# Moving score banks, one V product and one statistics step in a four-layer transformer kernel

## The chip, the cores and the metric

The kernel runs on one core of a Trainium2 chip. The metric is the device time of one execution in microseconds, the median of several runs. Short names: PE is TensorE (PEld its weight loads), DVE is VectorE, ACT is ScalarE, POOL is GpSimd, SP the queue that issues the transfers.

## The reference, cut to what matters

Sixteen sequences of 256 tokens with 256 features go through four layers, each a conditioned attention block and a conditioned MLP block. Layer 1 is causal, layer 3 rotates q and k and has a gated MLP, layers 2 and 3 have biases on q, k and v.

```
for layer in (L0, L1, L2, L3):
    h = norm(x) * (1 + scale1) + shift1          # per sequence
    q, k, v = h @ Wq, h @ Wk, h @ Wv             # 16 heads of 16 features
    a = softmax(q @ k.T / 4)                     # layer 1: causal mask
    x = x + gate1 * ((a @ v) @ Wo)
    h = norm(x) * (1 + scale2) + shift2
    x = x + gate2 * (act(h @ W1 + b1) @ W2 + b2)
```

## The kernel before, in words

The program is a pipeline over 64 tiles (4 layers times 16 sequences; tile n is sequence n mod 16 of layer n // 16). `steps` runs a body for t = -2 to 65. In a step, tile t+1 (`s.q`) gets its q, k and v, tile t (`s.a`) its attention, tile t-1 (`s.r`) its output projection and second norm, and tile t-2 (`s.m`) its MLP. Of each layer the steps 3 to 13 are a hardware loop (`Fori`), the others are written out. Each engine runs its own instructions in the order of the code and waits on semaphores.

Within a step PE does the MLP of tile t-2 interleaved with the untransposed scores of tile t (`score_pair`, from which DVE takes the maxima), then `query`, `key`, and then the part that this document is about. There, the sixteen heads of tile t are done again as transposed scores: eight `transposed_pair`s, two at a time; the exponentials of ACT (L893, one per head, 512 columns, 384 in the causal layer) read them from the PSUM bank that `ST_BANKS` names for the head, and write the tile `PR`; `outputs(g)` multiplies the exponentials of heads 4g to 4g+3 with V (L701). Between them stand `values(0)` and `values(1)`, the two halves of the V projection of tile t+1, and `norm_2`, the transposes of the second norm of tile t-1. The order before, outside the last layer:

`transposed_pairs(0, 1)`, `maxima_to_rows(1)`, `key(0)`, `key(1)`, `transposed_pairs(2, 3)`, `outputs(0)`, `transposed_pairs(4, 5)`, `values(0)`, `outputs(1)`, `norm_2`, `transposed_pairs(6, 7)`, `outputs(2)`, `values(1)`, `outputs(3)`.

PSUM has 8 banks of 512 columns. `banks_free` makes PE wait for the exponential of the last head that used the bank (`ac_exp`), or, for a bank that had other contents, for the engine that reads those. Before, heads 0 to 7 use banks 4, 5, 0, 7 twice, and heads 8 to 15 use 4, 5, 1, 3 twice, so heads 2 and 3 and heads 6 and 7 share banks 0 and 7. q is projected into bank 1, k into bank 3, v into bank 2; DVE evacuates them (`split_q` and `split_k` at L1315 to L1327, `values_out` at L1230). `up(j)` of the MLP takes banks 3 and 2 in turn.

DVE does after the last maxima: `split_q`, `split_k` (each a high part and a low part), `statistics_2` of the second norm (L935, L940), `normalise_2` (L948), which waits for the reciprocal root from POOL (L1358, L1360), `modulate_2` (L1116, L1125), then the evacuations of `outputs` (L1222) and of V (L1230). POOL makes the low part of the second norm's features from `modulate_2` (L1440), for which the first `up` of the next step waits. SP moves the rows of maxima into QS (L1484), for which pairs 0 and 4 wait, and stacks q and k into QS and KS (L1518).

Of the kernel before, what the change touches and what calls it, by code (L numbers as in the profile page):

```python
# [25 lines left out]
ACT = mybir.ActivationFunctionType  # L26
# [44 lines left out]
WO_BANK = 6  # L71
NORM1_BANK = 6

ST_BANKS = ((4, 5, 0, 7) * 2 + (4, 5, 1, 3) * 2, (4, 5, 0, 7) * 2 + (4, 5, 0, 1) * 2)
NORM2_BANK = (0, 7)
PARTNER = [i ^ HG for i in range(32)]

# [7 lines left out]
def build(nc, a, out):  # L85
    ctx = ExitStack()
    with ctx:
# [243 lines left out]
        def apart(eng):  # L331

            eng.nop(nofuse=True)

        def hidden_hi(eng, s, j):

            if s.lm == ROPE:
                eng.wait_ge(dv_gh, NJ * (s.m - NSEQ * ROPE) + j + 1)
            else:
                eng.wait_ge(ac_g, NJ * s.m + j + 1)  # L340
# [26 lines left out]
        def _(pe):  # L367
# [77 lines left out]
            def body(s):  # L445
# [49 lines left out]

                def up(j):

                    m, dst = s.m, bank(3 - j % 2)
                    x = H1 if isinstance(m, int) and m == NTILE - 1 else H2
                    if j == 0:  # L500
                        if x is H1:
                            pe.wait_ge(dv_g, NJ * (m - NSEQ * ROPE))
                        weights(s.lm, "1", s.sm, *((0, 4, 2, 6) if s.lm == ROPE else (0, 2)))
                        pe.wait_ge(dv_h2, m + 1)
                        pe.wait_ge(po_h2, m + 1)
                        key_read(s)
                    elif j == 1:
                        at_least(pe, dv_v, s.nq)
                    elif s.lm == ROPE:
                        pe.wait_ge(dv_g, NJ * (m - NSEQ * ROPE) + j - 1)  # L510
                    else:
                        pe.wait_ge(ac_g, NJ * m + j - 1)
                    if j == NJ // 2:
                        weights(s.lm, "1", s.sm, *((1, 5, 3, 7) if s.lm == ROPE else (1, 3)))
                    last = project(dst[:, 0, :], cols(W1, j * P), x)
                    if s.lm == ROPE:
                        last = project(dst[:, 1, :], cols(W1, DFF + j * P), x)
                    last.then_inc(pe_up, 1)
# [57 lines left out]
                def norm_2():  # L576

                    if s.a is not None:
                        pe.wait_ge(ac_exp, H * s.a + last_user(ST_BANKS[rope][0:HB] + (NORM2_BANK[rope],), HB) + 1)
                    pe.wait_ge(dv_xn2, s.r + 1)  # L580
                    to_features(bank(NORM2_BANK[rope]), TOK).then_inc(pe_h2, 1)

# [28 lines left out]
                def values(i):  # L611

                    if s.q is None:
                        return
                    if scored and i == 0:
                        pe.wait_ge(dv_max, H * (s.a + 1))
                    elif i == 0:
                        hidden_read(s)
                        at_least(pe, dv_v, s.nq)
                    for k in range(KD):  # L620
                        last = product(bank(2)[:, i, :], [x[:, k, i * P:(i + 1) * P] for x in H1],
                                       [w[:, k, 2 * D:3 * D] for w in wq], k == 0, k == KD - 1)
                    if i == NT - 1:
                        last.then_inc(pe_v, 1)
# [26 lines left out]
                def banks_free(p):  # L651

                    a_, banks = s.a, ST_BANKS[rope]
                    if p % HQ == 0:
                        pe.wait_ge(sp_mt[p // HQ], 16 * (a_ + 1))
                    for h in (2 * p, 2 * p + 1):
                        before = last_user(banks, h)
                        if before is not None:
                            pe.wait_ge(ac_exp, H * a_ + before + 1)
                        elif banks[h] in (0, 4, 5):  # L660
                            pe.wait_ge(dv_max, H * a_ + last_user(S_BANKS + (banks[h],), H) + 1)
                        elif banks[h] == 7:
                            at_least(pe, dv_dn, s.m_done)
                        elif banks[h] == 1 and rope:
                            pe.wait_ge(dv_rot, 2 * (s.q - NSEQ * ROPE) + 1)
                        elif banks[h] == 1:
                            at_least(pe, dv_q, s.q_done)
                        elif banks[h] == 3:
                            at_least(pe, dv_k, s.q_done)

                def transposed_pair(p):

# [101 lines left out]
                if scored:  # L774
                    transposed_pairs(2, 3)
                    outputs(0)
                    transposed_pairs(4, 5)
                    values(0)
                    if rope and s.r is not None:
                        norm_2()  # L780
                    outputs(1)
                    if not rope and s.r is not None:
                        norm_2()
                    transposed_pairs(6, 7)
                    if rope:
                        values(1)
                    outputs(2)
                    if not rope:
                        values(1)
                    outputs(3)  # L790
                else:
                    values(0)
                    values(1)
                    if s.r is not None and not s.tail:
                        norm_2()
# [10 lines left out]
        def _(ac):  # L806
# [24 lines left out]
            def body(s):  # L831
# [18 lines left out]
                for j in range(NJ) if s.m is not None else ():  # L850
# [7 lines left out]
                    at_least(ac, po_gl, NJ * m + j + 1 - RING)  # L858
                    if s.lm == ROPE:

                        nc.scalar.activation(G[:, j % RING, :], bank(3 - j % 2)[:, 1, :], ACT.Silu,
                                             bias=VEC[:, ROPE, V_B1 + NJ + j:V_B1 + NJ + j + 1]).then_inc(ac_g, 1)
                    else:

                        at_least(ac, pe_dn, NJ * m + j + 1 - RING)
                        for dst in (G, GH[0]):
                            last = nc.scalar.activation(dst[:, j % RING, :], bank(3 - j % 2)[:, 0, :], ACT.Gelu,  # L867
                                                        bias=VEC[:, s.lm, V_B1 + j:V_B1 + j + 1])
                        last.then_inc(ac_g, 1)
                    if j == 1:  # L870
# [61 lines left out]
        def _(dv):  # L932
# [85 lines left out]
            def body(s):  # L1018
# [16 lines left out]
                def hidden(j):  # L1035
                    m = s.m
                    if s.lm == ROPE:
                        dv.wait_ge(ac_g, NJ * m + j + 1)
                        nc.vector.scalar_tensor_tensor(G[:, j % RING, :], bank(3 - j % 2)[:, 0, :],  # L1039
                                                       VEC[:, ROPE, V_B1 + j:V_B1 + j + 1], G[:, j % RING, :],  # L1040
                                                       ALU.add, ALU.mult).then_inc(dv_g, 1)
                        dv.wait_ge(dv_g, NJ * (m - NSEQ * ROPE) + j + 1)
# [181 lines left out]
                def values_out():  # L1224
# [2 lines left out]
                        return  # L1227
                    dv.wait_ge(pe_v, s.q + 1)
                    at_least(dv, po_v, s.nq)
                    nc.vector.tensor_copy(VT[:], bank(2)).then_inc(dv_v, 1)  # L1230

                if s.tail:
                    return
# [20 lines left out]
                    evacuate(1)  # L1254
                else:
                    split_q()
                    split_k()
                    if s.lr != ROPE:
                        statistics_2()
                    normalise_2()  # L1260
                    modulate_2()
                    evacuate(0)
# [394 lines left out]
```

## Time and profile before

| | us |
|---|---|
| median of 3 runs | 2203.06 (2202.44 to 2203.37) |
| the profiled execution | 2201.76 |
| its span | 2199.6 |

| engine | busy us | share of the span |
|---|---|---|
| PE | 2124.3 | 97% |
| PEld | 1794.6 | 82% |
| DVE | 1711.1 | 78% |
| ACT | 1250.9 | 57% |
| POOL | 1043.9 | 47% |

The granted clock of TensorE is 0.99 of full speed over the span. Matmuls overlap in the pipeline and their ends are modelled, so PE's busy share hides short waits; they are read from the distances between the starts of matmuls and loads. The idle time in brackets behind a load is the time in which no load ran, which is also there when the matmuls before it take long, so it is compared with the same kind of place elsewhere.

### The profile page before, as it was taken

The page shows a single profiled execution, that of the slowest core. Times are in us where ns is not written, and L with a number is a line of the kernel's source. Part 1 is how long each engine was busy: PE and PEld are TensorE (multiplying, and loading weights), DVE is VectorE, ACT ScalarE, POOL GpSimd, SP SyncE. Part 2 cuts the span into 40 slices and gives each one's busy share as a digit, 9 for nine tenths or more (in the row PEclk, how much of TensorE's full clock was granted, in tenths as well). Part 3 has the DMA queues.
Part 4 walks back from the last instruction along what each step waited for, and adds up shares of the span by engine and source line. Part 5 has one row for each costly group of instructions (what it writes and reads, how often), then busy time and mean ns, then how long its engine had stood idle before and what let it go on. Part 6 is the DMA issues. An engine that isn't in the chain of part 4 may idle for free.

```text
span 2199.6 us, 63077 instructions
## 1 busy us (share of the span) xinstructions
PE 2124.3 (97%) x20080; PEld 1794.6 (82%) x20080; DVE 1711.1 (78%) x4340; ACT 1250.9 (57%) x2618; POOL 1043.9 (47%) x1300
## 2 busy tenths in 40 slices
PE   5899999999999999999999999999999999999998
PEld 4688888888888888888878887888888888888887
DVE  5677777777777777777777777777999898989884
ACT  1566666666655555555676666666655454444543
POOL 2345544555554455445455544545553434344433
PEclk8899999999999999999999999999999999999999
DMA  6421222222222212212332121122221212121210
GB/s 214 154 67 64 68 72 67 63 75 86 91 71 72 69 61 67 72 63 81 104 96 64 66 76 62 58 72 83 72 95 57 74 53 72 57 69 57 69 63 25
DMA packets 164143, 166.11 MB, mean 76 GB/s; under 512 B 28672, under 2 KB 143232, under 8 KB 164032
## 3 DMA queue, kind: packets, MB, share of 16 engines
q1 hardware_dynamic: 164032, 164.69, 23.3%
q8 instruction: 63, 1.03, 0.2%
q14 instruction: 48, 0.39, 0.1%
HBM read 58.47 MB, written 4.39 MB: 29 GB/s over the span
## 4 chain that ended last, share of the span: by engine, by line
PE 74%; DVE 12%; issue 5%; ACT 2%; POOL 2%; SPq 2%; DMA 1%; DVEq 0%; ACTq 0%; POOLq 0%
PE B L371 31%; PE B L532 14%; PE B L701 8%; PE B L678 6%; PE B L476 6%; DVE NEGM L1032 4%; PE B L541 4%; PE B L551 2%; ACT PR L893 2%; PE B L635 2%; PE B L449 2%; SPq L1518 2%; DVE ST L935 1%; DVE G L1039 1%; POOL GHl L1397 1%
## 5 line engine op out<-in xcount | busy, mean ns | idle before, releaser
L893 ACT ACTIVATE PR<-B 128x512 f32<-128x512 f32 (+1 forms) x1024 | 504.7, 571 | 284.1 <-PE B L678 279.2
L1397 POOL TENSOR_TENSOR GHl<-G,GHh 128x256 fp32r<-128x256 f32 x512 | 377.5, 738 | 452.2 <-ACT GHh L867 282.1
L1032 DVE TENSOR_REDUCE NEGM<-B 128x2 f32<-128x512 f32 x768 | 485.2, 682 | 80.4 <-PE B L476 80.3
L371 PE MATMUL B<-H2h,W1h 128*128 128x256 f32 x1248 | 387.7, 311 | 1.9 <-DVE VT L1230 1.2
L371 PE MATMUL B<-H2h,W1l 128*128 128x256 f32 x1248 | 353.4, 283 | 0.0
L371 PE MATMUL B<-H2l,W1h 128*128 128x256 f32 x1248 | 352.7, 283 | 0.0
L867 ACT ACTIVATE G<-B,VEC 128x256 f32<-128x256 f32 x384 | 182.0, 474 | 274.7 <-PE B L371 274.7
L532 PE MATMUL B<-W2h,GHh 128*128 128x256 f32 x1024 | 296.9, 290 | 4.4 <-POOL GHl L1397 2.9
L532 PE MATMUL B<-W2l,GHh 128*128 128x256 f32 x1024 | 290.1, 283 | 0.0
L532 PE MATMUL B<-W2h,GHl 128*128 128x256 f32 x1024 | 289.3, 283 | 0.0
L371 PEld LDWEIGHTS B<-H2h,W1h 128*128 128x128 f32 x1248 | 237.3, 190 | 43.6 <-issue 23.8
L701 PE MATMUL B<-PR,V 128*32 128x256 f32 (+1 forms) x4096 | 260.9, 373 | 5.9 <-ACT PR L893 1.9
L371 PEld LDWEIGHTS B<-H2l,W1h 128*128 128x128 f32 x1248 | 238.2, 191 | 0.0
L371 PEld LDWEIGHTS B<-H2h,W1l 128*128 128x128 f32 x1248 | 237.2, 190 | 0.0
L678 PE MATMUL B<-QS,KS 64*128 64x256 f32 (+1 forms) x2048 | 200.5, 307 | 12.1 <-DMA QS<-MT 4.6
L678 PEld LDWEIGHTS B<-QS,KS 64*128 64x128 f32 x2048 | 142.8, 188 | 80.1 <-ACT PR L893 36.0
L532 PEld LDWEIGHTS B<-W2h,GHh 128*128 128x128 f32 x1024 | 195.4, 191 | 14.0 <-POOL GHl L1397 3.8
L476 PE MATMUL B<-KS,QS 48*128 48x256 f32 (+1 forms) x2048 | 194.9, 309 | 10.5 <-DVE NEGM L1032 5.5
L1029 DVE CUSTOM_DVE_ANT_0 B<-B,MASK 128x128 f32<-128x128 f32 (+1 forms) x512 | 165.8, 390 | 39.6 <-PE B L476 39.6
L532 PEld LDWEIGHTS B<-W2h,GHl 128*128 128x128 f32 x1024 | 195.9, 191 | 0.0
L532 PEld LDWEIGHTS B<-W2l,GHh 128*128 128x128 f32 x1024 | 195.9, 191 | 0.0
L701 PEld LDWEIGHTS B<-PR,V 128*32 128x32 f32 x4096 | 108.3, 110 | 89.9 <-ACT PR L893 19.6
(177 smaller groups left out, 4671.2 us busy)
## 6 DMA issues: line engine op xcount, KB each, us to landing
QS<-QHL SPq DMA_DIRECT2D x768, 64.0 KB, 2.1
KS<-KHL SPq DMA_DIRECT2D x768, 64.0 KB, 2.1
GA<-gate_scratch SPq DMA_DIRECT2D x48, 256.0 KB, 3.2
GM<-gate_scratch SPq DMA_DIRECT2D x48, 256.0 KB, 3.3
RAW<-in_w SPq DMA_DIRECT2D x36, 256.0 KB, 3.2
GA<-in_rows_last SPq DMA_DIRECT2D x16, 256.0 KB, 3.1
GM<-in_rows_last SPq DMA_DIRECT2D x16, 256.0 KB, 3.1
out<-X SPq DMA_DIRECT2D x16, 256.0 KB, 2.2
```

The source lines that it names most:

```text
L371: last = nc.tensor.matmul(dst, w[i], x[j], start=(first_k and n == 0), stop=(last_k and n == 2))
L449: return nc.tensor.matmul(dst, IDENTB[:], MASK[:, 1], start=True, stop=False, skip_group_check=True)
L476: last = nc.tensor.matmul(bank(banks[h])[:, i, 0:keys], QS[b:b + STK, p, i * P:(i + 1) * P], KS[b:b + STK, p, 0:keys], start=True, stop=True)
L532: last = nc.tensor.matmul(bank(7)[:, i, :], GH[x][:, j % RING, i * P:(i + 1) * P], W2[y][:, j, :], start=(j == 0 and n == 0 and i == 0), s ...
L541: last = nc.tensor.transpose(dst[:, f, i * P:(i + 1) * P], src[:, i, f * P:(f + 1) * P], IDENT[:])
L678: last = nc.tensor.matmul(B[:, banks[h], k * T:k * T + T - first], KS[b:b + ROWS, p, k * P:(k + 1) * P], QS[b:b + ROWS, p, first:T], start ...
L701: last = nc.tensor.matmul(bank(6 + g // 2)[32 * j:32 * j + 32, g % 2, c], V[:, k, HV * h:HV * h + 32], PR[:, h % PRING, k, 0:n], start=(k ...
L867: last = nc.scalar.activation(dst[:, j % RING, :], bank(3 - j % 2)[:, 0, :], ACT.Gelu, bias=VEC[:, s.lm, V_B1 + j:V_B1 + j + 1])
L893: nc.scalar.activation(PR[:, h % PRING].rearrange("p k q -> p (k q)")[:, 0:n], src[:, 0:n], ACT.Exp, scale=SCALE).then_inc(ac_exp, 1)
L1029: last = nc.vector.tensor_tensor_reduce(src[:, i, 0:keys], src[:, i, 0:keys], unmasked, -1.0, HIGHEST, ALU.add, ALU.min, NEGM[:, i, c:c + 1])
L1032: last = nc.vector.tensor_reduce(NEGM[:, :, c], src, op=ALU.max, axis=AX.X, negate=True)
L1397: nc.gpsimd.tensor_tensor(GH[1][:, j % RING, :], G[:, j % RING, :], GH[0][:, j % RING, :].bitcast(F32), ALU.subtract).then_inc(po_gl, 1)
```

## The change

Four things, all of them outside the last layer (`rope` and `s.la == ROPE` keep the code before; the last attention step, t = 63, takes the new banks too, since it has no next tile):

- Banks: the heads 0 to 15 use 4, 5, 0, 7, 4, 5, 1, 2, and the same again. Heads 4 to 7 go to 4, 5, 1, 2 and wait for exponentials 0 and 1 and for q's evacuation from bank 1. `norm_2`, in bank 0, now waits for exponential 10.
- `values(0)` stands behind `outputs(1)`, and V is projected into bank 3, where k was, with a wait for k's evacuation (`dv_k`).
- `up(j)` takes banks 2 and 3 in turn, not 3 and 2; the wait for k's evacuation moves from `up(0)` to `up(1)`.
- `statistics_2` stands between `split_q` and `split_k` on DVE.

```
-ST_BANKS = ((4, 5, 0, 7) * 2 + (4, 5, 1, 3) * 2, (4, 5, 0, 7) * 2 + (4, 5, 0, 1) * 2)
+ST_BANKS = ((4, 5, 0, 7, 4, 5, 1, 2) * 2, (4, 5, 0, 7) * 2 + (4, 5, 0, 1) * 2)
+V_BANK = (3, 2)
...
+        def up_bank(s, j):
+
+            return 3 - j % 2 if s.la == ROPE else 2 + j % 2
...
-                        key_read(s)
+                        if s.la == ROPE:
+                            key_read(s)
                     elif j == 1:
+                        if s.la != ROPE:
+                            key_read(s)
                         at_least(pe, dv_v, s.nq)
...
-                        pe.wait_ge(ac_exp, H * s.a + last_user(ST_BANKS[rope][0:HB] + (NORM2_BANK[rope],), HB) + 1)
+                        pe.wait_ge(ac_exp, H * s.a + last_user(ST_BANKS[rope][0:12] + (NORM2_BANK[rope],), 12) + 1)
...
-                    if scored and i == 0:
+                    if i == 0 and rope:
                         pe.wait_ge(dv_max, H * (s.a + 1))
                     elif i == 0:
+                        pe.wait_ge(dv_k, s.q + 1)
+                    if i == 0 and not scored:
                         hidden_read(s)
                         at_least(pe, dv_v, s.nq)
...
-                        elif banks[h] == 3:
-                            at_least(pe, dv_k, s.q_done)
+                        elif banks[h] == 2:
+                            pe.wait_ge(dv_max, H * (a_ + 1))
...
                     transposed_pairs(4, 5)
-                    values(0)
-                    if rope and s.r is not None:
-                        norm_2()
+                    if rope:
+                        values(0)
+                        if s.r is not None:
+                            norm_2()
                     outputs(1)
-                    if not rope and s.r is not None:
-                        norm_2()
+                    if not rope:
+                        values(0)
+                        if s.r is not None:
+                            norm_2()
...
                     split_q()
-                    split_k()
                     if s.lr != ROPE:
                         statistics_2()
+                    split_k()
                     normalise_2()
```

PE, in the loop of the first layer, before: heads 4 and 5, heads 6 and 7, and the first product with V (QS,KS are transposed scores, PR,V the product with V, IDENT,TOK `norm_2`, WQ0h,H1h the V projection).

```order
L678 MATMUL B<-QS,KS 128x256 [waits ac_exp]
L678 MATMUL B<-QS,KS 128x256 x3
L659 REGISTER_ALU
L678 MATMUL B<-QS,KS 128x256 [waits ac_exp]
L678 MATMUL B<-QS,KS 128x256 x3
L691 REGISTER_ALU [waits po_v,ac_exp]
```

The same place in the changed kernel:

```order
L688 MATMUL B<-QS,KS 128x256 [waits ac_exp]
L688 MATMUL B<-QS,KS 128x256 x3
L688 MATMUL B<-QS,KS 128x256 [waits dv_max,dv_q]
L688 MATMUL B<-QS,KS 128x256 x3
L701 REGISTER_ALU [waits po_v,ac_exp]
```

The second pair (heads 6 and 7) no longer waits for an exponential, but for DVE. PE a little later in the same step, before: heads 10 and 11, then the V projection's six products (the last is shown), the second product with V, and `norm_2`.

```order
L678 MATMUL B<-QS,KS 128x256 [waits dv_k,dv_q]
L678 MATMUL B<-QS,KS 128x256 x3
L371 MATMUL B<-WQ0h,H1h 128x256 [waits dv_max]
...
L371 MATMUL B<-WQ0h,H1l 128x256
L701 MATMUL B<-PR,V 32x256 [waits ac_exp]
L701 MATMUL B<-PR,V 32x256 x7
L579 REGISTER_ALU
L541 MATMUL B<-IDENT,TOK 128x128 [waits dv_xn2,ac_exp]
```

The same place in the changed kernel:

```order
L688 MATMUL B<-QS,KS 128x256 [waits ac_exp]
L688 MATMUL B<-QS,KS 128x256 x3
L711 MATMUL B<-PR,V 32x256 [waits ac_exp]
L711 MATMUL B<-PR,V 32x256 x7
L376 MATMUL B<-WQ0h,H1h 128x256 [waits dv_k]
...
L376 MATMUL B<-WQ0h,H1l 128x256
L549 MATMUL B<-IDENT,TOK 128x128 [waits dv_xn2,ac_exp]
```

The product with V now directly follows the transposed scores, and `norm_2` the V projection. DVE in the same loop, before: the two halves of `split_k` and then `statistics_2` and `normalise_2`.

```order
L1327 TENSOR_TENSOR QHL<-B,QHL 128x512 [waits dv_qh]
L1325 CAST KHL<-B 128x512 [waits sp_stk1,sp_stk0,pe_k]
L1327 TENSOR_TENSOR KHL<-B,KHL 128x512 [waits dv_kh]
L935 ISA [waits po_x1]
L935 BN_STATS ST<-X 128x6
...
L940 BN_AGGR MV<-ST 128x2
L948 TENSOR_SCALAR TOK<-X,MV,RS 128x256 [waits po_x2,po_rs2]
```

The same place in the changed kernel:

```order
L1340 TENSOR_TENSOR QHL<-B,QHL 128x512 [waits dv_qh]
L948 ISA [waits po_x1]
L948 BN_STATS ST<-X 128x6
...
L953 BN_AGGR MV<-ST 128x2
L1338 CAST KHL<-B 128x512 [waits sp_stk1,sp_stk0,pe_k]
L1340 TENSOR_TENSOR KHL<-B,KHL 128x512 [waits dv_kh]
L961 TENSOR_SCALAR TOK<-X,MV,RS 128x256 [waits po_x2,po_rs2]
```

The statistics stand ahead of k's evacuation instead of behind it. The instructions of ACT, POOL and SP and their waits are the same in both kernels.

## Rows read from the trace of the kernel before

**Rows 1.** Windows, busy time in one step of layer 0: PE, PEld, DVE, ACT, POOL, clock.
```profile
287.50:318.82 31.32, 31.06 (x299) 26.03 (x297) 23.38 (x46) 20.07 (x43) 15.80 (x19) 1.00 0.21 68
```
**Rows 2.** Timeline, PEld, same step: start, length, instructions [idle before, releaser].
```profile
309.82 0.30 PEld L678 LDWEIGHTS B<-QS,KS 64*128 64x128 f32 x4
310.41 0.33 PEld L678 LDWEIGHTS B<-QS,KS 64*128 64x128 f32 x4 [0.29 <-ACT PR L893]
...
311.87 0.53 PEld L678 LDWEIGHTS B<-QS,KS 64*128 64x128 f32 x8 [0.41 <-ACT PR L893]
312.54 0.19 PEld L371 LDWEIGHTS B<-WQ0h,H1h 128*128 128x128 f32 x1
...
313.45 0.59 PEld L701 LDWEIGHTS B<-PR,V 128*32 128x32 f32 x16
314.45 0.42 PEld L541 LDWEIGHTS B<-IDENT,TOK 128*128 128x128 f32 x4 [0.41 <-ACT PR L893]
315.03 0.54 PEld L678 LDWEIGHTS B<-QS,KS 64*128 64x128 f32 x8 [0.17 <-issue]
...
317.77 0.59 PEld L701 LDWEIGHTS B<-PR,V 128*32 128x32 f32 x16 [0.29 <-ACT PR L893]
318.77 0.19 PEld L371 LDWEIGHTS B<-H2h,W1h 128*128 128x128 f32 x1 [0.41 <-issue]
```
**Rows 3.** Timeline, ACT, same step, exponentials 2 and 3, 5 and 6, 7, 12 to 15.
```profile
309.25 1.04 ACT L893 ACTIVATE PR<-B 128x512 f32<-128x512 f32 x2
...
310.86 1.08 ACT L893 ACTIVATE PR<-B 128x512 f32<-128x512 f32 x2
...
311.81 0.62 ACT L893 ACTIVATE PR<-B 128x512 f32<-128x512 f32 x1
...
315.65 2.07 ACT L893 ACTIVATE PR<-B 128x512 f32<-128x512 f32 x4 [1.10 <-PE B L678]
```
**Rows 4.** Timeline, PEld, a step of layer 2: the transposes of `norm_2`.
```profile
1274.59 0.42 PEld L541 LDWEIGHTS B<-IDENT,TOK 128*128 128x128 f32 x4 [0.75 <-ACT PR L893]
```
**Rows 5.** Timeline, DVE, the same step of layer 2.
```profile
1268.56 0.88 DVE L1320 SCALAR_TENSOR_TENSOR QHL<-B,VEC,QHL 128x256 fp32r<-128x256 f32 x2
1269.73 0.88 DVE L1315 TENSOR_SCALAR KHL<-B,VEC 128x256 fp32r<-128x256 f32 x2 [0.29 <-PE B L371]
...
1271.44 0.74 DVE L935 BATCH_NORM_STATS2 ST<-X 128x6 f32 x2
...
1273.73 0.73 DVE L948 TENSOR_SCALAR TOK<-X,MV,RS 128x256 f32 x2 [1.20 <-POOL RS L1360]
```
**Rows 6.** Timeline, PEld, a step of layer 1: masks of heads 4 to 7 and 8 to 11.
```profile
819.78 0.12 PEld L449 LDWEIGHTS B<-MASK,IDENTB 128*128 128x128 bf16 x2
820.15 0.13 PEld L449 LDWEIGHTS B<-MASK,IDENTB 128*128 128x128 bf16 x2 [0.25 <-ACT PR L893]
...
821.95 0.34 PEld L449 LDWEIGHTS B<-MASK,IDENTB 128*128 128x128 bf16 x4 [0.27 <-ACT PR L893]
```
**Rows 7.** Timeline, PE, layer 3: V projection's first product, `norm_2`, `outputs(1)`.
```profile
1776.16 0.39 PE L371 MATMUL B<-WQ1h,H1h 128*128 128x256 f32 x1
...
1776.98 0.60 PE L541 MATMUL B<-IDENT,TOK 128*128 128x128 f32 x4
1777.50 1.07 PE L701 MATMUL B<-PR,V 128*32 128x256 f32 x16
```
**Rows 8.** Waits of PE in layer 2, 1053.67 to 1533.44 us: total, times, longest.
```profile
PE B L541 <- DVE TOK L948: 4.8, 15, 0.7
```
**Rows 9.** Timeline, SP: the second rows of maxima. Tile QS: issue to landing.
```profile
308.95 0.56 SPq L1484 DMA_DIRECT2D QS<-MT  x1
...
DMA to landing us min/median/max: 2.0/2.1/2.4
```
**Rows 10.** Timeline, POOL, the step of Rows 2: low part for the next `up`.
```profile
317.08 1.28 POOL L1440 TENSOR_TENSOR H2l<-HF,H2h 128x512 fp32r<-128x512 f32 x1 [3.56 <-DVE H2h L1125]
```
**Rows 11.** Timeline, PE, last attention step (t = 63): `outputs(3)`.
```profile
2154.18 1.07 PE L701 MATMUL B<-PR,V 128*32 128x256 f32 x16 [0.91 <-ACT PR L893]
```

More of the change, by code:

```diff
@@ L496, in up @@
                 def up(j):
-                    m, dst = s.m, bank(3 - j % 2)
+                    m, dst = s.m, bank(up_bank(s, j))
                     x = H1 if isinstance(m, int) and m == NTILE - 1 else H2
@@ L620, in values @@
                     for k in range(KD):
-                        last = product(bank(2)[:, i, :], [x[:, k, i * P:(i + 1) * P] for x in H1],
+                        last = product(bank(V_BANK[rope])[:, i, :], [x[:, k, i * P:(i + 1) * P] for x in H1],
                                        [w[:, k, 2 * D:3 * D] for w in wq], k == 0, k == KD - 1)
@@ L859, in body @@
                     if s.lm == ROPE:
-                        nc.scalar.activation(G[:, j % RING, :], bank(3 - j % 2)[:, 1, :], ACT.Silu,
+                        nc.scalar.activation(G[:, j % RING, :], bank(up_bank(s, j))[:, 1, :], ACT.Silu,
                                              bias=VEC[:, ROPE, V_B1 + NJ + j:V_B1 + NJ + j + 1]).then_inc(ac_g, 1)
@@ L866, in body @@
                         for dst in (G, GH[0]):
-                            last = nc.scalar.activation(dst[:, j % RING, :], bank(3 - j % 2)[:, 0, :], ACT.Gelu,
+                            last = nc.scalar.activation(dst[:, j % RING, :], bank(up_bank(s, j))[:, 0, :], ACT.Gelu,
                                                         bias=VEC[:, s.lm, V_B1 + j:V_B1 + j + 1])
@@ L1038, in hidden @@
                         dv.wait_ge(ac_g, NJ * m + j + 1)
-                        nc.vector.scalar_tensor_tensor(G[:, j % RING, :], bank(3 - j % 2)[:, 0, :],
+                        nc.vector.scalar_tensor_tensor(G[:, j % RING, :], bank(up_bank(s, j))[:, 0, :],
                                                        VEC[:, ROPE, V_B1 + j:V_B1 + j + 1], G[:, j % RING, :],
@@ L1229, in values_out @@
                     at_least(dv, po_v, s.nq)
-                    nc.vector.tensor_copy(VT[:], bank(2)).then_inc(dv_v, 1)
+                    nc.vector.tensor_copy(VT[:], bank(V_BANK[s.lq == ROPE])).then_inc(dv_v, 1)
                 if s.tail:
```

## The prediction, made before the changed kernel was run

> **What bounds the kernel now.** I read first the busy times, then one step in the timeline of each layer, then who waits for whom. PE is the bound outside the last layer: in one step of layer 0 of 31.32 us it is busy for 31.06, at the full clock (1.00, which is 2.4 GHz), while DVE has 23.38 and ACT 20.07 [rows 1]. So a gain can only come from waits that the busy share hides, or from fewer changes of PE's way of working. To find them, the starts of the loads are compared with each other. An idle figure in brackets is no wait by itself: 0.41 us stand behind every product with V, since its short loads are through before its matmuls are. The waits in the part that changes are these. Heads 6 and 7 wait for exponential 3 (their banks are those of heads 2 and 3): the load at 310.41 has 0.29 us of idle time ascribed to ACT [rows 2]. `outputs(3)` waits for exponential 15, 0.29 us [rows 2]. In layer 2, `norm_2` has 0.75 us of idle time where layer 0 has 0.41 [rows 2, 4]: 0.34 us more, and in that layer the waits list has PE waiting for DVE's normalised tokens in 15 of 16 steps [rows 8]. The last layer keeps its code, so its part of the time only shifts.
>
> **The change, part by part, on the step of layer 0.** Two distances are needed first. From the end of an exponential to what waits for it: exponential 3 ends at 309.25 + 1.04 = 310.29 and the scores' load starts at 310.41, 0.12 later; exponential 15 ends at 315.65 + 2.07 = 317.72 and the load of `outputs(3)` starts at 317.77, 0.05 later [rows 2, 3].
>
> Banks. Heads 4 and 5 start at 309.82 as before; heads 6 and 7 follow at once, for banks 1 and 2 are free (the last maximum is already waited for by `maxima_to_rows(1)`; q's evacuation I check below). Two pairs take 312.54 - 311.87 = 0.67, so `outputs(0)` starts at 310.49, and a product with V takes 314.45 - 313.45 = 1.00 [rows 2]. PE is at heads 8 to 11 at 311.49 instead of 311.87. They now wait for exponential 5, which starts at 310.86 and takes 0.60 to 0.62; with 0.12 that is 311.6 [rows 3]. Their rows of maxima were sent at 308.95 and such transfers land after 2.0 to 2.4 us, by 311.35 [rows 9]: in time. They end at 311.6 + 0.67 = 312.27.
>
> Order. Now `outputs(1)` comes at once, and needs exponential 7. It starts at 311.81 and ends at 312.43 [rows 3], and nothing that moves is ahead of it: ACT has run without a break since its copy of the maxima. `outputs(1)` is the same kind of load as `outputs(3)`, so I take 0.05, not 0.12: it starts at 312.48. So of the 0.38 us that the banks give, 0.21 are lost again to a new wait. Then 1.00 for the product, 313.48 for `values(0)`, and 0.82 from there to the transposes, as in the last layer where these two stand in this order [rows 7]; before, the V projection took 313.45 - 312.54 = 0.91 to the product behind it. This 0.09 is a change of mode less: projection and transposes both use the whole array, while scores use half of its rows and the product with V quarters of its columns. `norm_2` starts at 314.30; from it to the next block it is 0.52 behind a projection [rows 7] and 0.58 behind a product with V [rows 2]; I take 0.55. So heads 12 to 15 start at 314.85 instead of 315.03. Their exponentials move along with them, and with them `outputs(3)` and the next step: **0.18 us less per step**. The cover holds: the next `up` needs POOL's low part, done at 317.08 + 1.28 = 318.36 against a start at 318.77 [rows 2, 10], and both move by 0.15 to 0.18. Layer 0 has 15 steps like this (t = 1 to 15): 15 x 0.18 = 2.7 us.
>
> The Trainium skill says in "TensorEngine Tiling (Array Packing)", Key Properties, that a change of the tiling mode, not of the tile, drains the array. By that rule alone, at the 0.09 us of the rows and with four changes of mode before and three after, a step would gain 0.09 and 46 steps 4.1 us; the waits are the larger part of my sum.
>
> Layer 1 (causal). Before, the masks of heads 4 to 7 take from 819.78 to 820.28, 0.50 us, those of heads 8 to 11 only 0.34 [rows 6]: 0.16 us of waiting for exponential 3, which goes. The exponentials have 384 columns there and end sooner against PE, so I expect no new wait, and the change of mode adds 0.09: 0.25 us in 16 steps, 4.0 us. If the new wait takes all of the 0.16, it is 1.4.
>
> Statistics between the splits, layer 2. q's low part ends at 1268.56 + 0.88 = 1269.44. Before, k's split starts at 1269.73, the statistics at 1271.44, and they are done 1.20 us ahead of the 1273.73 at which DVE normalises, so at 1272.53: 1.09 us [rows 5]. Now they run from 1269.44 to 1270.53, POOL has the root by 1271.73, and k's split (1.71 to 1.79) ends at 1272.3. Normalising runs from there to 1273.1, where `norm_2` is due at 1274.59 - 0.34 - 0.15 = 1274.1 [rows 4]. So its wait of 0.34 goes whole: 0.34 + 0.18 = 0.52 us in 15 steps, 7.8 us. k's evacuation comes 0.8 us later than before; behind it wait `values(0)`, due at 1273.3, and the stacking of k on SP, which follows six transfers of q. Both have about 1 us to spare. q's evacuation, for which bank 1 waits, is done at 1269.44, 0.4 before heads 6 and 7. In layers 0 and 1 the earlier statistics hide: there `norm_2` doesn't wait for DVE.
>
> `up` with banks 2 and 3 exchanged costs nothing: `up(0)` needs bank 2 read by exponential 14, and `outputs(3)` ahead of it has waited for 15. `norm_2` needs exponential 10, a microsecond before it. The last attention step takes the new banks too; ACT sets its end (0.91 us of waiting at `outputs(3)` [rows 11]). Between 0.2 and 0.9, I take 0.5.
>
> **Sum:** 2.7 + 4.0 + 7.8 + 0.5 = 15.0 us. The profiled execution took 2201.76 us, 1.30 less than the median of the runs, so it becomes 2186.8 and the median 2203.06 - 15.0 = 2188.1 us.
>
> **The rivals.** *ACT keeps the pace.* If `outputs(1)` can't start before 312.66, 0.23 after exponential 7 ends, the new wait eats all of the banks' and the order's gain in layer 0 (0 us), in layer 1 only the 0.09 stays (1.4 us), and in layer 2 the 0.34 (5.1 us): 6.5 us, 2196.6. For it speaks that ACT runs its exponentials 1 to 11 nearly without a break; against it the 0.05 and 0.12 us of the rows.
>
> *POOL's root waits for DVE.* It now runs beside k's split, where DVE was idle before. If it can't start before 1272.3, it is there at 1273.5, the tokens at 1274.25 and `norm_2` some 0.26 late: 3.9 us less gain, 2192.0. Against it: POOL's low part ran from 317.08 beside DVE's evacuations and took its usual 1.28 [rows 10]. The Trainium skill, "SBUF — State Buffer", Who interferes with whom, says that casts and tensor_scalars of DVE can take the port pair that POOL shares, and then the later one blocks; k's split begins with such an instruction.
>
> *It doesn't do what it says.* Heads 6 and 7 then wait for DVE instead of ACT, and `norm_2` still for the tokens; only the change of mode stays: 46 x 0.09 = 4.1 us, 2199.0, within 0.2%. The 0.4 us and 1.0 us to spare speak against it.
>
> *Slower.* `values(0)` was 0.91 us of cover between heads 8 to 11 and `outputs(1)`. Now any lateness of exponential 7 stands on PE's path. With an average gain of 15.0 / 47 = 0.32 us per step, the kernel is level when it comes 0.32 later than now, at 312.75, and slower by more than 0.2% (4.4 us) from 312.85. At 0.6 us late, which is one exponential more ahead of it, the step would lose 0.28: 47 x 0.28 = 13 us, 2216. Nothing in the order of ACT changed, so I see no reason for it.
>
> **Chances.** Forecast 68%, ACT's pace 12%, POOL's wait 7%, not as it says 8%, slower 5%. The forecast's own bounds: 0.11 to 0.21 per step by the distances, 1.4 to 4.0 in layer 1, 0.2 to 0.9 at the end: 2184 to 2193. With waits that go beyond what the rows show, 2181. The range 2181 to 2197 takes in the first three cases. A measurement of this kernel can tell about 0.2% from no change: faster 87%, within 0.2% 8%, slower 5%.
>
> **What would show it.** Right: no idle time by ACT ahead of heads 6 and 7; a new one of 0.2 to 0.3 us ahead of `outputs(1)`; steps of 31.14 us in layer 0, and in layer 2 steps shorter by 0.5 us; the wait for the tokens gone from the list. Wrong: an idle time over 0.4 us ahead of `outputs(1)`, PE waiting for DVE at heads 6 and 7 or `values(0)`, or steps of layer 2 shorter by less than 0.3 us.

## The result, and the profile after

| | us |
|---|---|
| before, median of 4 runs | 2203.11 (2202.44 to 2203.37) |
| after, median of 4 runs | 2186.49 (2185.01 to 2188.44) |
| ratio | 0.9922, 95% interval 0.991 to 0.9934 |
| profiled execution of after, and its span | 2186.55, 2184.3 |

The changed kernel is 16.6 us faster; 15.0 were predicted. The page of after: engines' busy time, share of the span, instructions.

```profile
PE 2111.2 (97%) x20080; PEld 1791.1 (82%) x20080; DVE 1704.5 (78%) x4340; ACT 1249.3 (57%) x2618; POOL 1046.0 (48%) x1300
```

PE has 13.1 us less of "busy" with the same 20080 matmuls: as said of [rows 1], the waits that go were hidden inside the modelled busy time. So the place is read from starts again. Timeline of PEld in after, the step of layer 0 that answers to [rows 2]:

```profile
310.14 0.54 PEld L688 LDWEIGHTS B<-QS,KS 64*128 64x128 f32 x8
310.81 0.59 PEld L711 LDWEIGHTS B<-PR,V 128*32 128x32 f32 x16
311.88 0.57 PEld L688 LDWEIGHTS B<-QS,KS 64*128 64x128 f32 x8 [0.48 <-ACT PR L906]
312.79 0.59 PEld L711 LDWEIGHTS B<-PR,V 128*32 128x32 f32 x16 [0.35 <-ACT PR L906]
313.79 0.19 PEld L376 LDWEIGHTS B<-WQ0h,H1h 128*128 128x128 f32 x1 [0.41 <-issue]
...
314.50 0.46 PEld L549 LDWEIGHTS B<-IDENT,TOK 128*128 128x128 f32 x4
315.13 0.53 PEld L688 LDWEIGHTS B<-QS,KS 64*128 64x128 f32 x8 [0.17 <-issue]
...
317.87 0.59 PEld L711 LDWEIGHTS B<-PR,V 128*32 128x32 f32 x16 [0.30 <-ACT PR L906]
318.87 0.19 PEld L376 LDWEIGHTS B<-H2h,W1h 128*128 128x128 f32 x1 [0.41 <-issue]
```

Heads 4 to 7 are now one row of eight loads without a gap. Ahead of the second product with V there is a new wait: the exponentials (timeline of ACT, first those of heads 4 and 5, then those of heads 6 and 7) end at 310.68 + 1.08 = 311.76 and at 311.65 + 1.09 = 312.74, and what needs them starts 0.12 and 0.05 us later.

```profile
310.68 1.08 ACT L906 ACTIVATE PR<-B 128x512 f32<-128x512 f32 x2
```
```profile
311.65 1.09 ACT L906 ACTIVATE PR<-B 128x512 f32<-128x512 f32 x2
```

Counted from the load of heads 4 and 5, with before by [rows 2]:

| start of | before | forecast | after |
|---|---|---|---|
| heads 8 to 11 | 2.05 | 1.78 | 1.74 |
| `outputs(1)` | 3.63 | 2.66 | 2.65 |
| `values(0)` | 2.72 | 3.66 | 3.65 |
| heads 12 to 15 | 5.21 | 5.03 | 4.99 |
| next `up` | 8.95 | 8.77 | 8.73 |

Layer 2, in place of [rows 4 and 5]: PEld around the second norm's transposes, then DVE, then POOL's root.

```profile
1263.80 0.19 PEld L376 LDWEIGHTS B<-WQ0h,H1h 128*128 128x128 f32 x1 [0.41 <-issue]
...
1264.51 0.46 PEld L549 LDWEIGHTS B<-IDENT,TOK 128*128 128x128 f32 x4
1265.14 0.54 PEld L688 LDWEIGHTS B<-QS,KS 64*128 64x128 f32 x8 [0.17 <-issue]
```
```profile
1259.88 0.74 DVE L948 BATCH_NORM_STATS2 ST<-X 128x6 f32 x2
1260.73 0.25 DVE L953 BATCH_NORM_AGGREGATE MV<-ST 128x2 f32<-128x6 f32 x2
1260.89 0.87 DVE L1328 TENSOR_SCALAR KHL<-B,VEC 128x256 fp32r<-128x256 f32 x2
1261.80 0.87 DVE L1333 SCALAR_TENSOR_TENSOR KHL<-B,VEC,KHL 128x256 fp32r<-128x256 f32 x2
1262.60 0.73 DVE L961 TENSOR_SCALAR TOK<-X,MV,RS 128x256 f32 x2
```
```profile
1261.14 0.22 POOL L1371 TENSOR_SCALAR TV<-MV 128x2 f32<-128x2 f32 x1 [2.63 <-DVE MV L953]
1261.44 0.71 POOL L1373 TENSOR_TENSOR RS<-TV,HALF 128x2 f32<-128x2 f32 x1
```

The tokens are ready at 1263.33, 1.2 us before the transposes at 1264.51; before, they were the last thing to arrive. The root (done at 1262.15) hides behind k's evacuation. The waits of PE in layer 2 no longer hold the row of [rows 8]; what is left of it:

```profile
PE B L549 <- DVE TOK L1292: 2.8, 3, 1.0
PE B L711 <- ACT PR L906: 0.5, 3, 0.2
```

Layer 1, PEld, in place of [rows 6]: the masks of heads 4 to 7 take 0.33 us, not 0.50; the wait ahead of those of heads 8 to 11 is unchanged.

```profile
816.39 0.33 PEld L454 LDWEIGHTS B<-MASK,IDENTB 128*128 128x128 bf16 x4
...
818.41 0.35 PEld L454 LDWEIGHTS B<-MASK,IDENTB 128*128 128x128 bf16 x4 [0.27 <-ACT PR L906]
```

A step's length, from the first `up` of one step to that of the next, repeats within 0.06 us inside a layer's loop, and its median within 0.02 us between the two profiles of the changed kernel, much better than whole runs do. It is the measure for all that follows. Where the 15.3 us between the two spans lie:

| stretch | before | after | difference | forecast |
|---|---|---|---|---|
| loop step, layer 0 / 1 / 2 | 31.34 / 31.96 / 31.81 | 31.10 / 31.62 / 31.24 | -0.24 / -0.34 / -0.57 | -0.18 / -0.25 / -0.52 |
| steps 2 to 15 | 439.15 | 435.85 | -3.3 | -2.5 |
| steps 16 to 31 | 514.86 | 510.34 | -4.5 | -4.0 |
| steps 32 to 46 | 479.77 | 470.92 | -8.9 | -7.8 |
| last attention step (t = 63) | 37.93 | 37.09 | -0.8 | -0.5 |
| start to the end of step 1 | 99.60 | 101.34 | +1.7 | -0.2 |
| the rest | | | +0.5 | 0 |

### The profile page after: what moved, and what is told of

The parts are those of the page before. It is cut to its first block, busy times and chain, and to the rows that moved or that the text cites. A ratio compares the mean times of both kernels' runs of the same rounds, so it can differ in the third digit from the quotient of the medians.

```text
span 2184.3 us, 63124 instructions
## 1 busy us (share of the span) xinstructions
PE 2111.2 (97%) x20080; PEld 1791.1 (82%) x20080; DVE 1704.5 (78%) x4340; ACT 1249.3 (57%) x2618; POOL 1046.0 (48%) x1300
## 4 chain that ended last, share of the span: by engine, by line
PE 74%; DVE 10%; issue 5%; ACT 4%; SPq 2%; DMA 2%; POOL 1%; ACTq 1%; DVEq 0%; POOLq 0%
PE B L376 31%; PE B L540 14%; PE B L711 8%; PE B L481 6%; PE B L688 6%; DVE NEGM L1045 4%; ACT PR L906 4%; PE B L549 3%; PE B L559 2%; SPq L1531 2%; PE B L645 2%; PE B L454 2%; DMA RAW<-in_w 1%; DVE G L1052 1%; POOL GHl L1410 1%
## 5 line engine op out<-in xcount | busy, mean ns | idle before, releaser
L1453 POOL TENSOR_TENSOR H2l<-HF,H2h 128x512 fp32r<-128x512 f32 x63 | 81.0, 1285 | 263.6 <-DVE H2h L1138 263.6
L688 PE MATMUL B<-QS,KS 64*128 64x256 f32 (+1 forms) x2048 | 191.2, 302 | 8.1 <-DMA QS<-MT 3.3
```

Of the source, the lines that this page charges most:

```text
L688: last = nc.tensor.matmul(B[:, banks[h], k * T:k * T + T - first], KS[b:b + ROWS, p, k * P:(k + 1) * P], QS[b:b + ROWS, p, first:T], start ...
L1453: nc.gpsimd.tensor_tensor(H2[1][:], HF[:], H2[0][:].bitcast(F32), ALU.subtract).then_inc(po_h2, 1)
```

## The experiments

All are the kernel before or the changed kernel with one edit, or with two where the text says so. Ratios are to the kernel before, run beside them on the same chip, where its median was between 2203.1 and 2204.3 us. The table has them all, with the median length of the loop steps. "Banks, order" is the changed kernel with the statistics taken back, "banks, statistics" the one with the order taken back.

| kernel | layer 0 | layer 1 | layer 2 | median, us | ratio (95%) |
|---|---|---|---|---|---|
| before | 31.34 | 31.96 | 31.81 | 2203.1 | |
| statistics only | 31.34 | 32.00 | 31.87 | 2206.0 | 1.0005 (0.9995 to 1.0015) |
| order only | 31.30 | 31.83 | 31.81 | 2200.6 | 0.9989 (0.998 to 0.9999) |
| banks only | 31.30 | 31.75 | 31.81 | 2201.2 | 0.999 (0.9981 to 1.0) |
| banks, order | 31.30 | 31.63 | 31.80 | 2198.7 | 0.9977 (0.9968 to 0.9987) |
| banks, statistics | 31.04 | 31.73 | 31.30 | 2189.1 | 0.9938 (0.9918 to 0.9958) |
| all three (after) | 31.10 | 31.62 | 31.24 | 2186.5 | 0.9922 (0.991 to 0.9934) |
| all three, again | 31.10 | 31.60 | 31.23 | 2186.3 | 0.9923 (0.9906 to 0.994) |
| after, 2 small exponentials | 31.29 | 31.60 | 31.38 | 2190.8 | 0.9952 (0.9935 to 0.9968) |
| after, 6 small exponentials | 31.63 | 31.67 | 31.75 | 2203.6 | 1.0 (0.9991 to 1.001) |
| before, 2 small exponentials | 31.32 | 31.97 | 31.77 | 2202.7 | 0.9996 (0.9987 to 1.0006) |
| before, 6 small exponentials | 31.33 | 31.96 | 31.76 | 2202.1 | 0.9995 (0.9985 to 1.0005) |
| banks turned | 31.11 | 31.53 | 31.25 | 2185.9 | 0.9927 (0.991 to 0.9943) |
| banks turned, norm ahead | 30.84 | 31.53 | 31.25 | 2179.9 | 0.9899 (0.9882 to 0.9915) |

**The statistics, taken back and alone.** Against the changed kernel:

```
                     split_q()
+                    split_k()
                     if s.lr != ROPE:
                         statistics_2()
-                    split_k()
```

> The changed kernel with the statistics of the second norm behind k's evacuation again, all else as changed. Theory (what the earlier statistics save is the wait of the second norm's transposes for the normalised tokens, and since those transposes now come earlier, they would wait longer for them): layer 2 gives back 0.54 us in 15 steps, 8.1 us; in layer 0 the tokens would be there at 8.65 us of the step against 8.64 for the transposes and a start 0.15 behind them, so 0.16 us in 15 steps, 2.4 us; layer 1 nothing. 2186.5 + 10.5 = 2197.0 us. Rival (the statistics are worth what the wait was before, 0.34 us in the steps of layer 2): 2191.6 us.

(Times "of the step" count from the first load of `query`.)

Measured: 2198.7 us; layer 2 longer by 0.56 us a step, layer 0 by 0.20, layer 1 by 0.01. The theory holds, and the rival falls. PEld of that kernel in layer 2 shows the transposes alone waiting again, 0.55 us, although behind a V projection there is no gap there otherwise; DVE's tokens are the cause (the row ascribes it to ACT, but DVE's row, behind it, has the tokens end at 1270.94 + 0.74 = 1271.68, 0.11 before the load).

```profile
1271.06 0.19 PEld L376 LDWEIGHTS B<-WQ0h,H1l 128*128 128x128 f32 x1
1271.79 0.42 PEld L549 LDWEIGHTS B<-IDENT,TOK 128*128 128x128 f32 x4 [0.55 <-ACT PR L906]
```
```profile
1270.94 0.74 DVE L961 TENSOR_SCALAR TOK<-X,MV,RS 128x256 f32 x2 [1.21 <-POOL RS L1373]
```

The same exchange of lines in the kernel before, alone:

> The kernel before with the statistics between the two evacuations alone. Theory (they free the transposes of layer 2 from their wait, 0.34 us in 15 steps, and nothing in layers 0 and 1): 2203.1 - 5.1 - 0.4 for the steps at the layer's ends = 2197.6 us. Rival (the root of POOL or k's evacuation becomes late, so that the gain stays out): 2201 to 2203 us.

Measured: 1.0005, and layer 2 is longer by 0.06, not shorter by 0.34. My theory missed, and the rival has the cause right; the kernel is even a little slower than its 2201 to 2203. PEld in layer 2:

```profile
1275.69 0.30 PEld L678 LDWEIGHTS B<-QS,KS 64*128 64x128 f32 x4 [0.41 <-ACT PR L893]
1276.28 0.33 PEld L678 LDWEIGHTS B<-QS,KS 64*128 64x128 f32 x4 [0.29 <-issue]
...
1277.65 0.59 PEld L701 LDWEIGHTS B<-PR,V 128*32 128x32 f32 x16
1278.65 0.42 PEld L541 LDWEIGHTS B<-IDENT,TOK 128*128 128x128 f32 x4 [0.41 <-ACT PR L893]
```
```profile
1275.29 0.88 DVE L1320 SCALAR_TENSOR_TENSOR KHL<-B,VEC,KHL 128x256 fp32r<-128x256 f32 x2
```

The transposes have lost their wait (0.41 where it was 0.75), but heads 10 and 11 now start 0.59 us behind heads 8 and 9, with 0.29 of idle time: their bank is 3 in the old table, k's bank, and k's evacuation ends only at 1276.17. The wait has moved from the tokens to the scores. The earlier statistics need the new banks, in which no head waits for k.

**The order alone, and the order taken back.** The V projection behind the second product with V in the kernel before (V still in bank 2):

```
-                    values(0)
-                    if rope and s.r is not None:
-                        norm_2()
+                    if rope:
+                        values(0)
+                        if s.r is not None:
+                            norm_2()
                     outputs(1)
-                    if not rope and s.r is not None:
-                        norm_2()
+                    if not rope:
+                        values(0)
+                        if s.r is not None:
+                            norm_2()
```

> The kernel before with the V projection behind the second product with V alone, V in bank 2 as before, old banks. Theory (a change of mode less in each step, and against it the wait for exponential 7, which in the old banks comes later by the 0.3 us that PE waits for exponential 3): layer 0 0.05 us less in 15 steps, layer 1 0.14 to 0.21 less in 16 steps, layer 2 nothing while the tokens are late: 2199.3 us (2198.5 to 2200.5). Rival (the mode change is worth 0.09 in every step): 2203.1 - 46 x 0.09 = 2199.0 us in sum, but then with 0.09 in every layer and not only where PE didn't wait. Rival that it costs: 2203 us or more.

Measured: 0.9989, steps shorter by 0.04, 0.13 and 0.00: the theory's pattern, not 0.09 in every layer. The same edit undone in the changed kernel:

> The changed kernel with the old order (V projection, second product with V, second norm's transposes), all else as changed, V in bank 3. Theory (the order brings a change of mode less, but in layer 0 the wait for exponential 7, which goes with the old order; in layer 2 the V projection would wait for k's evacuation, done at 6.70 us of the step): layer 0 0.07 us shorter in 15 steps, -1.0; layer 1 0.21 longer in 16, +3.3; layer 2 0.18 longer in 15, +2.7: 2186.5 + 5.0 = 2191.5 us. Rival (the order is worth its mode change alone, 0.09 x 46): 2190.6 with the same 0.09 in all three layers. Rival (the order is what brings the gain of the banks to the end): over 2195 us.

Measured: 2189.1 us. By the steps, the order costs 0.06 us in layer 0 and brings 0.12 in layer 1 and 0.06 in layer 2. The sign in layer 0 is as the theory has it; in layers 1 and 2 it is worth less than expected (0.21, 0.18). In layer 2 the V projection does wait for k's evacuation: it starts 0.84 us behind the scores of heads 8 to 11 where layer 0 has 0.70, and these 0.14 less the 0.07 of layer 0 are about what is measured. Summed over the layers the order is worth about 2 us of the 16.6. The medians alone (2191.5 and 2190.6 expected) could not tell the theory from the first rival; the steps do.

**The banks alone.** The edit just made (old order) and the one ahead of it (statistics behind k's evacuation), both in the changed kernel; what stays of the change is the banks:

> The kernel before with the new banks alone (V in bank 3 and up's banks exchanged with them), the V projection ahead of the second product with V as before, the statistics behind k's evacuation as before. Theory (banks and statistics need each other: the banks bring PE to the second norm's transposes earlier than the tokens are there when the statistics stand behind): in layer 0 the transposes could start at 8.51 us of the step but the tokens come at 8.65 and 0.15 later they start, 8.80 as before: 31.33 us, nothing gained; layer 1 31.73, 0.23 less in 16 steps, 3.6 us; layer 2 31.80, nothing. 2203.1 - 3.6 = 2199.5 us. Rival (the banks are worth the 0.29 us of layer 0 by themselves): 2195 us or less.

Measured: 0.999; 31.30, 31.75 and 31.81 where 31.33, 31.73 and 31.80 were expected. PEld in layer 0:

```profile
313.39 0.59 PEld L711 LDWEIGHTS B<-PR,V 128*32 128x32 f32 x16
314.65 0.42 PEld L549 LDWEIGHTS B<-IDENT,TOK 128*128 128x128 f32 x4 [0.67 <-ACT PR L903]
```

1.26 us from the product with V to the transposes, 1.00 in [rows 2]: what the banks win is waited off at the tokens. So one by one the banks bring 0.04 us in layer 0 and nothing in layer 2, and the statistics nothing in layer 0 and a loss of 0.06 in layer 2; together they bring 0.30 and 0.51 us.

**Exponential 7 made late.** For two (and six) small exponentials of no use, in the changed kernel and in the kernel before:

```
+                        for i in range(2 if h == 6 and s.lq != ROPE else 0):
+                            nc.scalar.activation(SPARE2[:, i:i + 1], HALF[:, 0:1], ACT.Exp).then_inc(ac_table, 1)
```

> The changed kernel with two extra small exponentials on ACT (one column each, 0.20 us each, of no use) ahead of exponential 6 of every tile outside the last layer: exponential 7 comes 0.41 us later. Theory (nothing covers exponential 7 any more: the second product with V waits for it on PE's path): layers 0 and 2, whose PE waits for it already, lose 0.41 us in some 30 steps, 12.3 us; layer 1 has about 0.4 us of slack at that place and loses 0 to 0.1 in 16 steps: 2186.5 + 12.5 = 2199 us (2197 to 2201). Rival (ACT's lateness is taken up elsewhere): 2186.5 to 2190 us.

> The kernel before with the same two extra small exponentials ahead of exponential 6. Theory (the V projection stands as cover between heads 8 to 11 and the second product with V, so 0.41 us of lateness is hidden there, in layer 0 0.37 us of it wholly): 2203.1 us, at most 2204.5. Rival (ACT's lateness costs PE in either kernel): 2213 us or more.

Measured: 2190.8 and 2202.7 us. The second is as expected. In the first, the steps of layers 0 and 2 are longer by 0.19 and 0.14, not by 0.41: I had added the durations of two instructions of 0.20 us that overlap. Two take 0.29 and six 0.66 us in the rows of ACT, 0.09 apart, so the exponential behind them was late by 0.18, and the second product with V with it. The dose was wrong, not the mechanism, so a larger one:

> The changed kernel with six small exponentials ahead of exponential 6; two of them delayed it by 0.19 us, so six by 0.56. Theory (any lateness of exponential 7 stands on PE's path in layers 0 and 2): steps of 31.66 us in layer 0 and 31.79 in layer 2, 0.56 x 31 = 17.4 us more, and in layer 1, where 0.46 us were to spare, 0.1 x 16 = 1.6: 2205.5 us, slower than before, as the prediction's point of 0.32 us per step says. Rival (part of it is taken up further on, at heads 12 to 15 or the end of the step): 2198 us or less.

> The kernel before with six small exponentials ahead of exponential 6, which comes 0.56 us later. Theory (the V projection covers exponential 7, which had ended 1.0 us ahead of the second product with V): nothing in any layer, 2203.1 us (up to 2205 if exponential 11, which then ends 0.1 us behind the start of heads 12 and 13, delays heads 14 and 15). Rival (ACT is near its limit there too): 2212 us or more.

Measured: after 2203.6, ratio 1.0; before 2202.1. Exponential 7 comes 0.53 us late, and the steps are longer by 0.53, 0.05 and 0.52 in the three layers. In the kernel before not one layer grows (layer 2 even shrinks by 0.04 with the small exponentials, which may be why the first dose shows 0.14 there and not 0.18). ACT and PEld of the changed kernel with six:

```profile
317.33 0.66 ACT L908 ACTIVATE SPARE<-HALF 128x1 f32<-128x1 f32 x6
```
```profile
317.56 0.56 PEld L689 LDWEIGHTS B<-QS,KS 64*128 64x128 f32 x8 [0.48 <-ACT PR L909]
319.02 0.59 PEld L712 LDWEIGHTS B<-PR,V 128*32 128x32 f32 x16 [0.89 <-ACT PR L909]
```

The idle time ahead of the second product with V has grown from 0.35 to 0.89. The level point is where the prediction's mechanism has it, but not where its sum put it: 0.53 us late, not 0.32, since layer 1 has 0.46 us to spare at that place and only 31 steps pay.

**Banks turned.** Heads 8 to 11 no longer wait for exponential 5:

```
-ST_BANKS = ((4, 5, 0, 7, 4, 5, 1, 2) * 2, (4, 5, 0, 7) * 2 + (4, 5, 0, 1) * 2)
+ST_BANKS = ((4, 5, 0, 7, 4, 5, 1, 2, 0, 7, 4, 5, 1, 2, 4, 5), (4, 5, 0, 7) * 2 + (4, 5, 0, 1) * 2)
```

> The changed kernel with other banks for heads 8 to 15 (0, 7, 4, 5, then 1, 2, 4, 5), so that heads 8 to 11 wait for exponentials 3 and 1 and not for 5. Theory (the second product with V still waits for exponential 7 right behind them, so what is won at heads 8 to 11 is lost there): 2186.5 us, within 1 us. Rival (the wait for exponential 5 costs by itself 0.10 us in 30 steps): 2183.5 us.

Measured: 0.9927; layers 0 and 2 as before the edit (31.11, 31.25), as expected; layer 1 shorter by 0.08, 1.3 us, which I had not: there nothing waits for exponential 7, so the 0.27 us ahead of the masks of heads 8 to 11 become 0.20 and the rest stays won.

```profile
816.74 0.33 PEld L454 LDWEIGHTS B<-MASK,IDENTB 128*128 128x128 bf16 x4 [0.20 <-ACT PR L906]
```

**Norm ahead: a faster version.** With the turned banks, and in layer 0 both the V projection and the transposes ahead of the second product with V. The transposes write bank 0, which heads 2 and 8 use in the turned table and heads 2 and 10 in that of the change, so with the turned banks they wait for exponential 8 and not for 10, which ends 0.98 us later:

```
-                    if rope:
+                    ahead = rope or s.la == 0
+                    if ahead:
                         values(0)
                         if s.r is not None:
                             norm_2()
                     outputs(1)
-                    if not rope:
+                    if not ahead:
```

> The kernel of banks_turned, and in layer 0 the order V projection, second norm's transposes, second product with V (layers 1 and 2 keep the changed order). Theory (with both in front of the second product with V, the wait for exponential 7 has cover and the mode changes are no more): heads 12 to 15 start at 8.9 us of the step in place of 9.17, 0.27 us in 15 steps: 2186.5 - 4.0 = 2182.5 us. Rival (the exponentials set the pace from there on, heads 12 to 15 must wait for exponential 11 or the third product with V for 15): 2186 us or more.

Measured: 0.9899, 2179.9 us; layer 0 is 0.27 us a step shorter than the kernel with the turned banks, as expected. That is 4.0 us; the medians are 6.0 apart, the profiled spans 4.3, with a start-up that is 1.1 us shorter and a last attention step 1.2 longer. PEld in layer 0:

```profile
308.94 0.53 PEld L688 LDWEIGHTS B<-QS,KS 64*128 64x128 f32 x8 [0.41 <-ACT PR L907]
309.60 0.19 PEld L376 LDWEIGHTS B<-WQ0h,H1h 128*128 128x128 f32 x1
...
310.41 0.42 PEld L549 LDWEIGHTS B<-IDENT,TOK 128*128 128x128 f32 x4
311.00 0.59 PEld L711 LDWEIGHTS B<-PR,V 128*32 128x32 f32 x16 [0.17 <-ACT PR L907]
312.00 0.53 PEld L688 LDWEIGHTS B<-QS,KS 64*128 64x128 f32 x8 [0.41 <-ACT PR L907]
```

From heads 8 to 11 to the product with V nothing waits by more than 0.1 us (the first load of the transposes comes 0.05 behind the end of exponential 8), and the product is followed by heads 12 to 15 after its usual 1.00. In layer 2 the V projection would wait for k's evacuation there, and layers 1 and 2 keep the changed order.

**The changed kernel again.**

> The changed kernel once more, as it is, beside the others. Theory: steps of 31.10, 31.62 and 31.24 us in layers 0, 1 and 2, as in its first profile, and 2186.5 us; the start-up up to step 1 (101.2 us in its first profile, 99.7 in that of the kernel before) and step 18 (33.8 against 33.3) vary from run to run, so here they should not come out the same. Rival (the start-up is longer because of the change): again 101 us or more, and 33.8 in step 18.

Measured: 0.9923, the same steps. The start until the end of step 1 took 101.4 us, step 18 33.9: by this run alone the rival would be right. The other profiles speak against it. Over all fourteen the start-up lies between 99.6 and 103.8 us, at 101.3 and 101.4 in those of the changed kernel and at 99.6, 100.2, 101.9 and 102.3 in four whose banks and order are those of before: no pattern. Step 18 is 0.8 to 2.5 us longer than step 17 in six profiles, and at most 0.1 in the other eight. The six are both of the changed kernel, the one with six small exponentials, the banks alone, and also "statistics only" and "before, 2 small exponentials", which have the old banks and the old order. Tile RAW, weights sent by SP around step 18, issue to landing, in before, after and "statistics only":

```profile
DMA to landing us min/median/max: 2.7/2.9/5.7
```
```profile
DMA to landing us min/median/max: 2.7/3.5/5.9
```
```profile
DMA to landing us min/median/max: 2.7/3.7/5.3
```

In the six the median landing takes 3.4 to 3.7 us, in the eight 2.8 to 3.1. In after, ACT waits 1.6 us for these weights instead of 0.5, and PE's wait for the first norm's tokens in that step grows from 1.1 to 1.9 us. So this varies between profiles, with the change and without it; why is open.

## Why the prediction was right, step by step

*Banks in layer 0.* Right: heads 6 and 7 follow at once, heads 8 to 11 start within 0.04 of the forecast, held by exponential 5.

*The new wait for exponential 7.* Right to 0.01 us (2.65 for 2.66). Taking 0.05 instead of 0.12 for the way from ACT to this load, because `outputs(3)` is the same kind of load, was the choice that mattered. The product starts 0.05 us behind exponential 7, not 0.23, so the rival "ACT keeps the pace" is out.

*The order.* Mis-sized. The 0.09 of [rows 2, 7] is the distance into the transposes: from the last matmul of the V projection there are 0.12 us to the start of the transposes and 0.21 to that of a product with V. Besides, the block behind the transposes follows 0.53 us after they begin, where I had taken 0.55. The forecast's 0.18 so becomes 0.22 at heads 12 to 15, and the loop step is 0.24 shorter, with 0.02 left over. But the runs also show that in layer 0 the order is a loss of 0.06 in all: the wait for exponential 7, 0.22 us, which it exposes, costs more than the change of mode and the shorter transposes save. I had summed both without asking whether this part of the change was worth having; the answer led to the faster version. The rule that I had cited from the Trainium skill, "TensorEngine Tiling (Array Packing)", Key Properties, that a change of the tiling mode drains the array, agrees with the direction (0.21 us where the mode changes, 0.12 where it does not), but by it alone all layers would gain alike, and they don't.

*Layer 1.* Forecast 0.25, measured 0.34. The 0.16 of the masks is right (0.50 became 0.33). The order is worth 0.12. The missing 0.07 stands ahead of the next `up`, which in layer 1 starts close behind POOL's low part. Before, POOL and PEld at the end of a step of layer 1:

```profile
827.43 1.29 POOL L1440 TENSOR_TENSOR H2l<-HF,H2h 128x512 fp32r<-128x512 f32 x1 [3.85 <-DVE H2h L1125]
```
```profile
828.11 0.59 PEld L701 LDWEIGHTS B<-PR,V 128*32 128x32 f32 x16
828.96 0.19 PEld L371 LDWEIGHTS B<-H2h,W1h 128*128 128x128 f32 x1 [0.27 <-issue]
```

After:

```profile
823.75 1.29 POOL L1453 TENSOR_TENSOR H2l<-HF,H2h 128x512 fp32r<-128x512 f32 x1 [5.84 <-DVE H2h L1138]
```
```profile
824.42 0.59 PEld L711 LDWEIGHTS B<-PR,V 128*32 128x32 f32 x16
825.21 0.19 PEld L376 LDWEIGHTS B<-H2h,W1h 128*128 128x128 f32 x1 [0.20 <-issue]
```

POOL's part ends 0.6 us behind the start of the last product in both, so it is no later before. But `up` starts 0.24 us behind POOL's end before and 0.17 after, and this goes by the banks: in the median of the layer's loop it is 0.23 in each of the five profiles with the old table and 0.16 to 0.19 in the nine with a new one, the banks alone among them. With the new tables `up(0)` takes bank 2 and no longer waits for k's evacuation; of this exchange I had written that it costs nothing, and it seems to be what brings the 0.07 (0.05 in the median of the loop steps). It was not run by itself.

*Statistics, layer 2.* The number is right (-0.57 for -0.52), the attribution is not. I wrote that the statistics take away norm_2's wait of 0.34 and that in layers 0 and 1 they hide. Alone they bring nothing, since k's evacuation, 0.64 us later (the prediction had 0.8), holds heads 10 and 11 in bank 3. And in layer 0 they are worth 0.20 us a step once the banks are new. The tokens were ready there just 0.15 us before the transposes started (8.65 and 8.80 us of the step). From DVE's tokens to transposes that wait for them there are 0.11 to 0.12 us (layer 2 before, and both layers with the statistics taken back), so they had 0.03 to 0.04 us of slack, and that is all that the banks alone win in layer 0. The sum came out because I had worked it out with all parts in place; its split, 2.7 + 4.0 + 7.8, is by layer and not by part of the change, and each of its terms was between 0.5 and 1.1 us too small.

*Exponential 10.* The prediction has it a microsecond ahead of `norm_2`, which waits for it. It ends 0.30 us ahead of the load, in layers 0 and 2. Nothing came of it here, but it is the next wait if the transposes move further ahead.

*POOL's root.* It ran its usual 0.22 and 0.71 us beside k's split, starting 0.25 us after it. The rule of the Trainium skill, "SBUF — State Buffer", Who interferes with whom, that such an instruction of DVE can block POOL, did not show here: POOL starts 0.16 us behind the end of the statistics before and after. This is no test of the rule in general, since k's split reads its input from PSUM.

*The last attention step.* -0.8 for -0.5 in this pair of profiles, -0.7 against the second profile of the changed kernel. The size is not shown: this step took 36.1 to 37.8 us in the nine profiles with new banks and 37.5 to 38.3 in the five with the old ones. What repeats is that the block of heads 4 to 7 is at least 0.5 us shorter in all nine.

*Slower.* The mechanism is confirmed, its price per microsecond too (1.0), its level point was too near: 0.53 us of lateness in place of 0.32. I had divided the gain by all 47 steps.

Against the medians, the forecast was 1.6 us too small; in the profiled executions the start-up (+1.7) and step 18 (+0.5) took 2.3 us back, which varies from profile to profile.

## What to carry to other kernels

Before an operation is moved earlier, look at every input of the operation behind it, those without a visible wait too: an input that is ready only just in time is a wait in waiting. Two edits that bring next to nothing one by one can bring most of the gain together, when each only moves the wait to what the other removes, so judge them as a set and then leave out each in turn. Where a long operation is taken away from between a producer's last result and its consumer, put another one there, if its own inputs are ready.

## What the runs showed of the hardware

Small ACT instructions in a row cost far less than their duration: exponentials of 128x1 take 0.20 us each in the rows, but six take 0.66 together and delay the next one by 0.53, 0.09 us each. From the end of an exponential to the load that waits for it there are 0.05 us at the product with V and 0.11 to 0.12 at the scores, the same in all profiles. From the V projection's last matmul the transposes start after 0.12 us, a product with V after 0.21. Four transposes behind a product with V take 0.38 us from the first start to the last. Behind a V projection they take 0.33 where their first load runs 0.10 ahead of its matmul, but 0.38 in the faster version, where that load waits for exponential 8 and is only 0.01 ahead. The same six weight transfers landed after a median of 2.8 to 3.7 us in fourteen profiles, in no order with the change.
